# Two half transposes and a value projection moved between the four runs of small matmuls in a slot

## The reference

```
for i in range(DEPTH):                                   # DEPTH = 6
    x = attn_layer(shift_tokens(x), Wqkv[i], q_scale[i], k_scale[i], Wo[i]) + x
    x = ffn_layer(shift_tokens(x), ln_g[i], ln_b[i], W1[i], b1[i], W2[i], b2[i]) + x

# attn_layer: 16 heads of 64 channels, windows of 32 tokens
q, k, v = split(x @ Wqkv)                                # 128 -> 3 x 1024
q = l2norm(q) * qs ; k = l2norm(k) * ksc                 # then a rotary embedding with a scale
sim = q @ [k of the window before, k of this window] * 8 # 32 queries x 64 keys, masked
out = softmax(sim) @ v                                   # of the same 64 tokens
return out @ Wo                                          # 1024 -> 128
```

## Time and profile before

| | us |
|---|---|
| median of three runs | 3939.11 (3936.31 to 3940.21) |
| the profiled execution | 3927.86 |
| its span, first to last instruction | 3926.1 |
| PE busy | 3686.9 (94% of the span) |
| DVE, POOL, ACT busy | 3008.4, 2597.5, 2270.5 |
| chain that ended last | PE 76%, issue 4%, POOL 3%, DVE 2% |

### The profile page before, as it was taken

The page is one execution under the profiler, slowest core; times in us unless marked ns, Lnnn a source line. Parts: engine busy times, 40 slices in busy tenths (PEclk is TensorE's granted clock), DMA queues, the critical chain, the costliest instruction groups (busy, mean ns, idle before and its releaser), DMA issues.

```text
span 3926.1 us, 163005 instructions
## 1 busy us (share of the span) xinstructions
PE 3686.9 (94%) x67712; PEld 2840.2 (72%) x67712; DVE 3008.4 (77%) x5061; ACT 2270.5 (58%) x4270; POOL 2597.5 (66%) x3029
## 2 busy tenths in 40 slices
PE   6999979999999999999999999999999999999998
PEld 3555547777767777668877677777677777778876
DVE  7666658878778788778887788877788887888876
ACT  3555546666546666456666466665466664566662
POOL 4545548777548787368887288775478874678870
PEclk8999989999999999999999999999999999999999
DMA  1000012222212222122222122222122221122220
GB/s 44 4 6 4 6 33 68 55 58 60 58 32 60 57 57 59 41 49 60 61 57 56 30 64 56 60 59 60 32 58 56 60 61 41 48 60 60 60 52 22
DMA packets 136307, 189.03 MB, mean 48 GB/s; under 512 B 38006, under 2 KB 58484, under 8 KB 135412
## 3 DMA queue, kind: packets, MB, share of 16 engines
q1 hardware_dynamic: 135540, 178.23, 17.7%
HBM read 22.67 MB, written 2.10 MB: 6 GB/s over the span
## 4 chain that ended last, share of the span: by engine, by line
PE 76%; issue 4%; POOL 3%; DVE 2%; ACT 0%; DMA 0%; POOLq 0%; SPq 0%; DVEq 0%; ACTq 0%
PE PS L1270 18%; PE PS L1417 10%; PE PS L1256 10%; PE PS L1294 8%; PE PS L1280 8%; PE PS L1257 8%; PE PS L1258 8%; PE PS L1476 2%; PE PS L1411 2%; PE PS L1454 1%; PE PS L1447 1%; POOL t L1182 1%; PE PS L1442 1%; POOL t L1187 1%; DVE m L1803 0%
## 5 line engine op out<-in xcount | busy, mean ns | idle before, releaser
L1182 POOL TENSOR_TENSOR t<-t 128x1024 f32<-128x1024 f32 x384 | 908.3, 2370 | 368.2 <-DVE t L1764 366.9
L1187 POOL TENSOR_TENSOR t<-t,rn 128x1024 f32<-128x1024 f32 x384 | 723.6, 1905 | 29.8 <-POOL rn L150 27.3
L1542 ACT ACTIVATE va<-PS 128x512 f32<-128x512 f32 x384 | 229.8, 598 | 631.9 <-PE PS L1258 631.6
L1763 DVE TENSOR_TENSOR t<-PS,rope 128x512 f32<-128x512 f32 x768 | 523.6, 682 | 27.9 <-ACT sq L1577 26.0
L1256 PE MATMUL PS<-w_hi,xh 128*128 128x512 f32 x1152 | 514.7, 447 | 22.8 <-DVE xl L1063 11.3
L1764 DVE TENSOR_TENSOR t<-PS,rope 128x512 f32<-128x512 f32 x768 | 522.9, 681 | 0.0
L1577 ACT ACTIVATE sq<-PS 128x512 f32<-128x512 f32 x768 | 454.2, 593 | 33.0 <-PE PS L1258 17.4
L1270 PE MATMUL PS<-constants,t 128*128 128x128 f32 x3072 | 443.3, 277 | 19.8 <-POOL t L1187 13.2
L1258 PE MATMUL PS<-w_lo,xh 128*128 128x512 f32 x1152 | 458.4, 398 | 0.0
L1257 PE MATMUL PS<-w_hi,xl 128*128 128x512 f32 x1152 | 458.3, 398 | 0.0
L1770 DVE TENSOR_REDUCE ss<-sq 128x16 f32<-128x1024 f32 x384 | 448.5, 1209 | 0.0
(11 more groups left out here) (167 smaller groups left out, 7697.7 us busy)
## 6 DMA issues: line engine op xcount, KB each, us to landing
vs<-va SPq DMA_DIRECT2D x768, 130.0 KB
vs<-va SPq DMA_DIRECT2D x768, 65.0 KB
t<-in_L_ffn_Wqkv SPq DMA_DIRECT2D x18, 512.0 KB, 4.5
w_out<-in_L_ffn_Wo SPq DMA_DIRECT2D x6, 512.0 KB, 3.9
a_normed<-in_L_attn_x SPq DMA_DIRECT2D x8, 256.0 KB, 6.4
a_xo<-in_L_attn_x SPq DMA_DIRECT2D x8, 256.0 KB, 2.9
out<-total SPq DMA_DIRECT2D x8, 256.0 KB, 3.5
w_raw<-in_L_ffn_W SPq DMA_DIRECT2D x6, 341.0 KB
```

The costliest lines, as they stand in the source:

```text
L1182: pool.tensor_tensor(mine[:, i, :], mine[:, i, :], t2[:, i, :], ALU.add).then_inc(done, 1)
L1187: pool.tensor_tensor(h, h, bc(rn[:, H * i:H * (i + 1)], 2, HB), ALU.mult).then_inc(done, 1)
L1763: dve.tensor_tensor(o1, src, bc(rope[:, 2 * i, t, :], 1, 8), ALU.mult)
```

## The change

On TensorE, the order of a full slot becomes: v0, k0, k1, q0, Tw0, q1, **mix0, Tw1**, Tq0, **v1**, mix1, **Tq1**, Tk0, Tm0, Tm1, masks, score0, **Tk1**, output projection, score1. Tw1 goes behind mix0, v1 ahead of mix1, Tq1 behind mix1, and Tk1 behind score0. The number of matmuls and transposes stays what it was. Since v1 comes earlier, it uses bank 5 instead of 6, behind the rope of k1, and Tq1 uses bank 6, behind the rope of q0 (`q_bank`; where nothing is projected, Tq1 keeps bank 5). Tm1, which writes bank 5, now waits for the copy of v1 too, and q0's projection into bank 6 waits for the qT copies of the slot before instead of the v copies.

On ScalarE the copy of v1 moves ahead of the copy of qT1. On VectorE the rope of q1 moves from behind both products `on` to between them (where age 2 is absent, it stays where it was).

```diff
                     if project_new:
-                        pe.wait_ge(rk_made, at(T, 0, 2, c + 1))
-                    turn(4 + c, lambda j: roped(0)(4 * c + j), qt_mm)
+                        if c == 0:
+                            pe.wait_ge(rk_made, at(T, 0, 2, 1))
+                        else:
+                            pe.wait_ge(rq_made, at(T, 0, 2, 1))
+                    turn(q_bank(project_new, c), lambda j: roped(0)(4 * c + j), qt_mm)
...
+                    if project_new and c == 1:
+                        pe.wait_ge(v_made, at(T, 0, 2, 2))
                     pe.wait_ge(on_made, at(T, 2, 2, c + 1))
...
-                    pe.wait_ge(v_made, at(T, 1, 2, 2))
+                    pe.wait_ge(qT_made, at(T, 2, 2, 2))
                     project(0, 0, 6, t, q_mm)
...
                 if mix:
-                    turn_weights(1)
                     pe.wait_ge(vs_in[tile2 % 2], VS_IN * (lay * (B * 2) + s2 * 2 + tile2 // 2) + VS_IN)
                     mix_half(0)
+                    turn_weights(1)
                 if score:
                     turn_q(0)
-                    turn_q(1)
+                if project_new:
+                    pe.wait_ge(rk_made, at(T, 0, 2, 2))
+                    project(2, 1, 5, t, v_mm)
                 if mix:
                     mix_half(1)
-                if project_new:
-                    pe.wait_ge(rq_made, at(T, 0, 2, 1))
-                    project(2, 1, 6, t, v_mm)
+                if score:
+                    turn_q(1)
...
-                    turn_k(1)
                     pe.wait_ge(on_made, at(T, 2, 2, 2))
...
                     score_half(0)
+                    turn_k(1)
...
                     turned_q(0)
+                if 0 in ages:
+                    values(lay, s, t, 1, 5)
+                if 1 in ages:
                     turned_q(1)
-                if 0 in ages:
-                    values(lay, s, t, 1, 6)
-                if 1 in ages:
                     turned_k(0)
...
+                if 0 in ages and not 2 in ages:
+                    rope_half(T, t, 0, 1, 7, sqq_made, qt_mm, addq_made, rq_made)
                 if 2 in ages:
                     for c in range(2):
+                        if 0 in ages and c:
+                            rope_half(T, t, 0, 1, 7, sqq_made, qt_mm, addq_made, rq_made)
...
                 if 0 in ages:
-                    rope_half(T, t, 0, 1, 7, sqq_made, qt_mm, addq_made, rq_made)
                     lengths(T)
```

More of the change, by code:

```diff
@@ L1018, in at, with q_bank @@
             return n * (T - back + CREDIT) + i
+        def q_bank(projecting, c):
+            return 4 if c == 0 else 6 if projecting else 5
         def room(s, t, back=0):
@@ L1623, in turned_q @@
                     act.wait_ge(qt_mm, at(T, 1, 2, c + 1))
-                    pairs(qT, c, 4 + c, qT_made)
+                    pairs(qT, c, q_bank(0 in ages, c), qT_made)
                 if ending:
```

## The result

The changed kernel takes 3993.38 us (four runs, 3984.72 to 4008.11), the kernel before beside it 3937.71: the ratio is 1.0154, 95% interval 1.0136 to 1.0172. That is slower, by 56 us between the medians and 61 us by the ratio, and outside the predicted range. The profiled execution took 4008.11 us against 3927.86 of before, 80 us more.

What follows compares the result with a forecast made beforehand. TensorE, busy 94% of the span, was taken as the bound, its idle time mostly late instruction blocks; 28 - 31 - 10 + 8 - 3 + 2 = -6 us gave a median of 3933 us, range 3900 to 3970 with rivals.

Steps and rivals of the forecast that it cites:

- Closing and ending slots: mix0 waits there for its copy without cover, +2 us: In closing and ending slots mix0 waits for the pT0 copy, Tw1 no longer ahead of it: +2 us.
- layer starts: At six layer starts Tw1 now covers a wait for GpSimd before Tq0: -3 us.
- undisturbed slot: A full slot without stalls or the Tm1 wait gets 0.07 us longer, +13 us over 180 slots.
- wait of Tm1: Tm1 waits 0.2 us for the second `on`, behind q1's rope on VectorE, in 105 slots unstalled in mix1: +21 us.
- stalls in mix1: Late instruction blocks inside mix1: in 75 of 180 full slots the stall falls from 1.1 to 0.62 us, -36 us.
- stalls in score1: Tk1 between score0 and score1 gives distance, 0.25 us less stall in 41 slots: -10 us.
- stalls in score0: score0 comes nearer to mix1, bringing new stalls of 0.1 us in some 80 slots: +8 us.
- A: Rival: block's time counts from the run's start, so mix1 stalls end 0.3 us earlier, score0 unstalled: 3903 us; chance 0.27.
- B: Rival: ScalarE's chain becomes the bound, Tm1 waits 0.4 us, score0 is held up: 3969 us; chance 0.16.
- C: Rival: stalls stay, as block arrival depends on something else; only costs remain, +49 us: 3988 us; chance 0.05.

Runs made afterwards that it cites:

- combined kernels: Kernel before, only full slots changed: v1, Tq1, Tk1 moved, Tw1 ahead of mix0, q1's rope last: ratio 1.0013; same with Tk1 ahead of the masks: 1.0016.
- the useless work: Kernel before with three extra transposes without use ahead of mix1 in each full slot: 3974.23 us against 3927.37, ratio 1.0119.
- the experiment on them: Changed kernel with Tw1 ahead of mix0 again in the six ending slots alone: 3975.22 us, ratio 1.0128 to the kernel before.

## Why the prediction was wrong

**The step that failed: "Closing and ending slots: mix0 waits there for its copy without cover, +2 us".** I priced one idle wait in twelve slots as a wait of VectorE's or ScalarE's size, and did not ask what covers mix1 and score1 where v1 and the output projection are absent. The wait ahead of mix0 grew in each of these twelve slots, a wait ahead of mix1 came in each ending slot and three closing ones, and one ahead of score1 in each first slot. They measured +25 us (closing and ending, with the feed-forward behind them) and +12 us (first slots, not in my sum at all; I had -3 for layer starts). Together this is 37 of the 61 us. A large part of it is not the idle time but the half clock behind it, which I had not considered, although the trace of before had it to show. How large is an estimate: between the two profiles the closing and ending slots and the feed-forward lost 40 us and have 69 us more at half clock, 27 us by the price of 2.6 for 6.7. But by the granted clocks of all executions the kernel with only these slots changed has 27 us more, which is 10 of its 25 us. In the first slots the larger share is idle time and the lost cover of Tk1.

**The full slots** were to gain some 7 us and lost 22. By terms, forecast and measured, all summed from start times:

| term | forecast | measured |
|---|---|---|
| undisturbed slot | +13 | +29 |
| wait of Tm1 | +21 | +21 |
| stalls in mix1 | -36 | -31 |
| stalls in score1 | -10 | -12 |
| stalls in score0 | +8 | +15 |
| layer starts, mix0 and other places | -3 | about 0 |

The order within the slot came out as worked out: mix0 starts 0.10 behind the copy pT0 (1555.52, 1555.62), mix1 2.51 later, the second product ends at 1560.40, Tm1 idles 0.2. The work behind mix0 is 9.54 where I had 9.53. The fault was the other end of the subtraction: I took 9.20 for before from the slot of the earlier trace rows, which holds 0.07 to 0.09 us of a stall; undisturbed it is 9.11. An error of 0.09 us is 16 us over 180 slots. The 22 us hold chance as well: the means of the four kernels with each order are 2613 and 2639 us, 26 apart. The term of score0 is right in size, but not shown to be a block that comes late: only 21 slots have a single gap over 0.1 us there, and 14 of the 15 us lie behind the 56th matmul of the run, in small steps, in 114 slots. The wait of Tm1 hardly shows in the view of waits (0.7 us in 2): transposes are drawn longer than their distance, so it must be read from start times.

**The rivals.** A falls: in the stalled slots mix1 resumes 3.6 us after mix0 began in the changed kernel (3.24 before), as the forecast had it, not 3.3. Counted from the end of the copy pT0 it is 3.6 before and 3.7 after. B's criterion, over 60 us of waiting for `on`, isn't met: 21 us. C's number, 3988, is near the result, but its mechanism is not: the stalls did fall, and line 1298's idle time is 39.5, below C's 55. By the "mostly hidden" of the page "Runtime: NRT & Kernel Launch" of the Trainium skill, section "Instruction fetch mechanics", the time would have been C's; the waits above, 39.5 us in 69 pieces, speak against that page after the change as before it.

**What was not seen about the gain.** I had reckoned stalls as a cost that distance removes. The combined kernels show that order alone removes little: with no added wait the sum of all excesses falls from some 120 us to 115 and 107, against 87 in the changed kernel, whose own waits (0.16 us ahead of mix0 and 0.2 ahead of Tm1) may give the blocks time, as the useless work did. Among kernels whose full slots have the very same order as before the sum of the full slots is 2622.5, 2616.8 and 2610.0 us, from where the stalls fall, and 2602.7 us where the longer first slots cover a wait as well. The 8 us by which the combined kernels lie under the first of these are within that scatter.

**What stays open.** Why the feed-forward has 20 to 25 us more at half clock even where the ending slots ahead of it have none; why the combined kernels, whose full slots and ends are no longer than before, still measure 5 and 7 us slower by the median, while their profiled executions are as long as that of before (3926.1 and 3925.0 us against 3926.1); how much the six ending slots alone cost, which the experiment on them left between 9 and 18 us; and what makes the end of score0 slow in the new order.

No kernel tried is faster than the one before.

## What to carry over

Before moving work out of a place, list every variant of the loop body that shares the code, above all those in which the neighbouring work is absent, and ask in each what now covers the wait. Price an idle wait of TensorE not only by its length but by the clock of the stretch behind it, which the windows show. Where the time at half clock differs between executions, take it from all of them and not from the profiled one alone. Where a term is multiplied by 180, take both sides of a difference from undisturbed slots, and take a minimum or a low percentile of many rather than one slot.

## What the runs showed of the hardware

The clock fell to half in slots whose idle stretches were no longer than 1.10, 0.79 and 0.84 us (the ending slot at 1631.7, granted clock 0.89 over the slot). One of six such slots kept the full clock (2772.8), and three of six in the kernel with only the closing and ending slots changed, so it isn't certain in each. Sixteen transposes in the idle places kept it full in all six. The stalls inside the runs fall where the count of instructions puts them: 64 waits without work moved all 64 stalls that can be compared by 16 matmuls, and three transposes in each full slot put a stall of 1.57 us (1.35 as drawn) into an ending slot, in which nothing had been edited.
